# Graph layer with a routed feed-forward: the routing of the node blocks follows the update chunk by chunk, with roots by a power on GpSimd and slots counted inside partitions first

## The reference, cut to what matters

```
xn = layernorm(x)
msg = silu(layernorm(silu([xn[src], xn[dst], d2] @ mW1 + mb1)) @ mW2 + mb2)      # per edge
agg = segment_sum(msg, src)
x   = x + xn + silu([xn, agg] @ uW1 + ub1) @ uW2 + ub2 + mix(xn)                 # per node, the "update"
xm  = layernorm(layernorm(x)) * gamma + beta                                      # the rows that are routed
logits = xm @ Wr + br                                                             # 8 experts
top two experts of each row, weights = softmax over the two
x   = x + sum over the two of weight * (gelu(xm @ W1[e] + b1[e]) @ W2[e] + b2[e])
```

## Time and profile before

| | |
|---|---|
| median of 3 runs | 1701.5 us (1700.61 to 1703.49) |
| the profiled execution | 1703.06 us, of which the span is 1701.3 us |
| PE / DVE / ACT / POOL busy | 90% / 72% / 58% / 51% of the span |
| edge loop ends, update begins | about 1318 us from the start of the span |
| update | 1318 to 1391 us |
| routing and slots | 1391 to 1436 us |
| experts | 1446 to 1665 us |

### The profile page before, as it was taken

One profiled execution on the slowest core, in us unless ns is written; L12 is line 12 of the kernel. 1 busy time (PEld: TensorE's weight loads), 2 busy tenths in 40 slices (PEclk: granted clock), 3 DMA queues, 4 the chain that ended last, 5 costly groups with the idle time before them and its releaser, 6 DMA issues.

```text
span 1701.3 us, 34990 instructions
## 1 busy us (share of the span) xinstructions
PE 1530.8 (90%) x8931; PEld 1277.9 (75%) x8932; DVE 1218.8 (72%) x4343; ACT 983.3 (58%) x2126; POOL 865.8 (51%) x1201
## 2 busy tenths in 40 slices
PE   5799969899789999999999999999999874999992
PEld 2499946455568999999999999999898653677771
DVE  6788662566248989999899989899896359344442
ACT  1022112244138888888888888888887342556551
POOL 3088872000316666666666666666661002566651
PEclk8555569999789999999999999999999987999996
DMA  4700001100102222222222222222364024344447
GB/s 161 109 5 4 5 23 51 34 1 1 49 26 74 73 74 71 74 74 71 74 71 74 73 72 72 73 74 71 71 75 162 0 94 191 59 67 68 68 60 242
DMA packets 62950, 118.69 MB, mean 70 GB/s; under 512 B 19927, under 2 KB 40965, under 8 KB 62390
## 3 DMA queue, kind: packets, MB, share of 16 engines
q0 software_dynamic: 36560, 77.56, 19.7%
q1 hardware_dynamic: 25616, 37.26, 7.3%
q10 hardware_dynamic: 720, 3.20, 0.5%
HBM read 92.79 MB, written 25.18 MB: 69 GB/s over the span
## 4 chain that ended last, share of the span: by engine, by line
PE 83%; DVE 7%; ACT 4%; issue 3%; DMA 2%; DVEq 0%; SPq 0%; ACTq 0%; POOLq 0%
PE ps L903 12%; PE ps L664 9%; PE ps L995 6%; PE ps L883 5%; PE ps L712 5%; PE ps L792 5%; PE ps L873 5%; PE ps L870 4%; PE ps L865 4%; PE ps L866 4%; PE ps L756 3%; PE ps L718 3%; PE ps L893 2%; PE ps L1022 2%; PE ps L1021 1%
## 5 line engine op out<-in xcount | busy, mean ns | idle before, releaser
L612 POOL DMA_INDIRECT msg_t<-dst_table,stage_idx x448 | 446.7, 997 | 106.0 <-issue 45.0
L903 PE MATMUL ps<-msg_t,hot_t 128*125 128x256 f32 x896 | 241.5, 392 | 14.1 <-issue 7.4
L1118 ACT ACTIVATE msg1n_t<-msg_t,nw_b,nw_y 128x256 f32<-128x256 f32 x448 | 243.7, 598 | 0.0
L578 POOL DMA_INDIRECT sorted_edges<-sort_sb_t,chunk_to x112 | 156.5, 1398 | 100.6 <-DVE chunk_to L1307 66.8
L1135 ACT ACTIVATE msg_t<-msg_t 128x512 f32<-128x512 f32 x224 | 141.5, 632 | 101.2 <-DVE msg_t L1495 101.2
L865 PE MATMUL ps<-w_hi_t,msg1T_hi_t 128*128 128x256 f32 x672 | 198.6, 310 | 0.0
L866 PE MATMUL ps<-w_lo_t,msg1T_hi_t 128*128 128x256 f32 x672 | 180.0, 282 | 0.0
L903 PEld LDWEIGHTS ps<-msg_t,hot_t 128*125 128x125 f32 x896 | 151.3, 188 | 32.1 <-issue 9.6
L883 PE MATMUL ps<-src_hi_t,hotT_t 127*128 x448 | 160.7, 379 | 3.7 <-ACT hotT_t L1131 3.7
L1495 DVE TENSOR_TENSOR msg_t<-ps,msg_t 128x512 f32<-128x512 f32 x224 | 152.8, 682 | 3.1 <-PE ps L883 3.0
L870 PE MATMUL ps<-w_hi_t,msg1T_lo_t 128*128 128x256 f32 x672 | 153.8, 283 | 0.0
(11 more groups left out here) (324 smaller groups left out, 3806.4 us busy)
## 6 DMA issues: line engine op xcount, KB each, us to landing
w_sb_t<-in_L_ffn_W_dram SPq DMA_DIRECT2D x16, 512.0 KB, 8.0
msg_t<-dst_table,stage_idx POOLq DMA_INDIRECT x448, 2.8
res_t<-in_x_dram SPq DMA_DIRECT2D x1, 3125.0 KB
total<-zero_chunks_t SPq DMA_DIRECT2D x1, 3125.0 KB, 29.2
dst_table<-dst_stage SPq DMA_DIRECT2D x25, 125.0 KB
xm_table<-xm_t POOLq DMA_DIRECT2D x5, 625.0 KB, 8.8
total<-res_t SPq DMA_DIRECT2D x1, 3125.0 KB
sum_b_t<-total ACTq DMA_DIRECT2D x5, 625.0 KB, 11.4
```

Of the source, the lines that this page charges most:

```text
L578: pool.indirect_dma_start(out=sorted_edges, out_offset=bass.IndirectOffsetOnAxis(chunk_to[:, g, j:j + 1], 0), in_=sort_sb[:, g, j].rearran ...
L612: pool.indirect_dma_start(out=msg1[:, k, j, :], out_offset=None, in_=dst_table, in_offset=bass.IndirectOffsetOnAxis(stage_idx[:, half, q:q ...
L903: m = pe.matmul(bank(7, D, rows=NP), hot[:, (k - 8) % TURN, j, 0:NP].bitcast(F32), msg2[:, k % 2, j, :], start=(j == 0), stop=(j == G - 1))
L1118: m = A(msg1n[:, (k + 1) % 2, j, :], msg1[:, kk, j, :], ACT.Identity, bias=nw_b[:, kk, j:j + 1], scale=nw_y[:, kk, j:j + 1])
```

## The change

1. `aggT`, `hidT`, `x2T` move to the space of the edge weights, so that `xm` can be written while the update runs.
2. The statistics of a chunk are turned into 1/root on POOL, as a power of -0.5 (`spread_of` on DVE makes the base, `pool.tensor_tensor(..., ALU.pow)`), instead of ACT's square root and DVE's reciprocal.
3. DVE copies the raw logits of block t-3 out of PSUM ahead of block t (`raw_logits`); PE's `route(t)` waits for the copy of block t-1. Bias, scaled logits and top two of chunk c-2 come behind chunk c (`pick`).
4. ACT normalises the blocks of chunk c-2 behind chunk c (`copy_xm`), and POOL stores the first piece behind the root of chunk 4.
5. Slots: DVE scans `hot_k` itself, so that the place inside a partition and the partition's count of each expert (`row_n`) are known, and PE sums only 8 columns over the partitions.
6. PE waits for `w2_rest` only before the first product with W2.

```
+            for c in range(len(CH)):
+                T = slice(CH[c][0], CH[c][-1] + 1)
+                pool.wait_ge(var2_ok, c + 1)
+                pool.tensor_tensor(rstd[0:NP, T], rstd[0:NP, T], minus_half[0:NP, 0:len(CH[c])], ALU.pow).then_inc(sd2_ok, 1)
+                if c >= len(CH) - 3:
+                    store_rows(c - len(CH) + 3)
+            for g in range(3, 5):
+                store_rows(g)
...
             def route(t):
                 pe.wait_ge(x2T_sb, t + 1)
+                after(pe, logit_ok, t)
...
-            flat = hot_k[0:NP].rearrange("p e m -> p (e m)")
-            pe.matmul(bank(3, NE * KT, rows=NP), earlier[0:NP, 0:NP], flat, start=True, stop=True)
-            pe.matmul(bank(4, NE * KT, rows=NP), ones[0:NP, 0:NP], flat, start=True, stop=True).then_inc(route_ps, 1)
+            pe.matmul(bank(3, NE, rows=NP), earlier[0:NP, 0:NP], row_n[0:NP, :], start=True, stop=True)
+            pe.matmul(bank(3, NE, rows=NP, first=NE), ones[0:NP, 0:NP], row_n[0:NP, :], start=True, stop=True)\
+              .then_inc(route_ps, 1)
...
-            pe.wait_ge(w2_rest_ok, NE)
...
                     pe.wait_ge(shT_sb, m_ + 1)
+                    if isinstance(m_, int) and m_ == 0:
+                        pe.wait_ge(w2_rest_ok, NE)
...
+            def copy_xm(c):
+                act.wait_ge(rstd2_ok, c + 1)
+                for t in CH[c]:
+                    A(xm[0:NP, t, :], res[0:NP, t, :], ACT.Identity, bias=nbias[0:NP, t:t + 1], scale=rstd[0:NP, t:t + 1])\
+                        .then_inc(xm_ok, 1)
...
                 for t in blocks:
                     if t >= 1:
                         copy_x2(t - 1)
+                if c >= 2:
+                    copy_xm(c - 2)
             copy_x2(NB - 1)
-            act.wait_ge(var2_ok, 1)
-            A(rstd[0:NP], meanvar[0:NP, :, 1], ACT.Sqrt, bias=eps2_col[0:NP, :], scale=1.0 + EPS).then_inc(sd2_ok, 1)
...
+            copy_xm(len(CH) - 2)
+            copy_xm(len(CH) - 1)
...
+            def raw_logits(t):
+                if t >= 0:
+                    dve.wait_ge(logit_ps, t + 1)
+                    dve.tensor_copy(logits[R, t, :], bank(7, NE, rows=NP, first=t * NE)).then_inc(logit_ok, 1)
...
+            def pick(c):
+                blocks, n = CH[c], len(CH[c])
+                T = slice(blocks[0], blocks[-1] + 1)
+                dve.wait_ge(sd2_ok, c + 1)
+                dve.wait_ge(logit_ok, blocks[-1] + 1)
+                dve.scalar_tensor_tensor(nbias[R, T], meanvar[R, T, 0], -1.0, rstd[R, T], ALU.mult, ALU.mult)\
+                   .then_inc(rstd2_ok, 1)
...
                 for t in blocks:
+                    raw_logits(t - 3)
                     dve.wait_ge(upd_ps, t + 1)
...
+                if c >= 2:
+                    pick(c - 2)
+                if 1 <= c < len(CH) - 1:
+                    spread_of(c - 1)
...
+            spread_of(len(CH) - 2)
+            spread_of(len(CH) - 1)
+            for t in range(NB - 3, NB):
+                raw_logits(t)
+            pick(len(CH) - 2)
+            pick(len(CH) - 1)
...
-            hc = hot_c[R].rearrange("p e m -> p (e m)")
-            step(dve.tensor_copy(hc, bank(4, NE * KT, rows=NP)))
...
+            step(dve.tensor_tensor_scan(hp, hk, hk, 0.0, ALU.add, ALU.bypass))
+            st.did(dve.tensor_copy(row_n[R, 0:1], hot_p[R, 0:1, KT - 1]))
+            step(dve.tensor_tensor(row_n[R, 1:NE], hot_p[R, 1:NE, KT - 1], hot_p[R, 0:NE - 1, KT - 1], ALU.subtract))
+            dve.tensor_copy(nw_t[R, 0, 0:1], row_n[R, 0:1]).then_inc(hotk_ok, 1)
...
-            step(dve.tensor_tensor(hp, hp, hc, ALU.subtract))
-            step(dve.tensor_tensor(hp, hp, bank(3, NE * KT, rows=NP), ALU.add))
```

More of the change, by code:

```diff
@@ L202, in gps_layer @@
         msg2 = at("msg2_t", [128, 2, G, D], F32, "work", 30720)
[L205 to L206 removed]
+        aggT = [at(f"aggT{i}", [128, KD, 4, NP], F32, "weights", 4096 * i) for i in range(2)]
+        hidT = [at(f"hidT{i}", [128, KD, 4, NP], F32, "weights", 8192 + 4096 * i) for i in range(2)]
+        x2T = [at(f"x2T{i}", [128, KD, NP], F32, "weights", 16384 + 1024 * i) for i in range(2)]
         xm = at("xm_t", [128, NB, D], F32, "work")
[L209 to L210 removed]
         w1_sb = at("w1_sb_t", [128, NE, KD, HID], F32, "src_hi")
@@ L633, in _, with store_rows @@
                       allow_small_or_imprecise_dtypes=True).then_inc(token_ok, 1)
-            for g in range(5):
+            def store_rows(g):
                 pool.wait_ge(xm_ok, 5 * (g + 1))
@@ L1170, in _ @@
                         copy_x2(t - 1)
+                if c >= 2:
+                    copy_xm(c - 2)
             copy_x2(NB - 1)
-            act.wait_ge(var2_ok, 1)
-            A(rstd[0:NP], meanvar[0:NP, :, 1], ACT.Sqrt, bias=eps2_col[0:NP, :], scale=1.0 + EPS).then_inc(sd2_ok, 1)
-            act.wait_ge(rstd2_ok, 1)
-            for t in range(NB):
-                A(xm[0:NP, t, :], res[0:NP, t, :], ACT.Identity, bias=nbias[0:NP, t:t + 1], scale=rstd[0:NP, t:t + 1])\
-                    .then_inc(xm_ok, 1)
+            copy_xm(len(CH) - 2)
+            copy_xm(len(CH) - 1)
             act.wait_ge(gap_ok, 1)
@@ L1537, in add_hidden, with spread_of @@
                 m.then_inc(hid_pre, 1)
+            def raw_logits(t):
+                if t >= 0:
+                    dve.wait_ge(logit_ps, t + 1)
+                    dve.tensor_copy(logits[R, t, :], bank(7, NE, rows=NP, first=t * NE)).then_inc(logit_ok, 1)
+            def spread_of(c):
+                T = slice(CH[c][0], CH[c][-1] + 1)
+                st.join()
+                dve.tensor_scalar(rstd[R, T], meanvar[R, T, 1], 1.0 + EPS, EPS * EPS, ALU.mult, ALU.add).then_inc(var2_ok, 1)
+            def pick(c):
[5 more added lines that the diff above has]
+                   .then_inc(rstd2_ok, 1)
+                step(dve.tensor_tensor(logits[R, T], logits[R, T], rstd[R, T].unsqueeze(2).broadcast_to([NP, n, NE]), ALU.mult))
+                step(dve.tensor_tensor(logits[R, T], logits[R, T], logit0[R].unsqueeze(1).broadcast_to([NP, n, NE]), ALU.add))
+                for t in blocks:
+                    st.did(dve.max(top_v[R, t, :], logits[R, t, :]))
+                st.join()
+                for t in blocks:
+                    st.did(dve.max_index(top_e[R, t, :], top_v[R, t, :], logits[R, t, :]))
             dve.wait_ge(mixed_ok, NB)
@@ L1559, in _ @@
             st.join()
-            dve.tensor_copy(nw_t[R, 0, 0:1], meanvar[R, 0, 0:1]).then_inc(var2_ok, 1)
-            dve.wait_ge(sd2_ok, 1)
-            step(dve.reciprocal(rstd[R], rstd[R]))
-            dve.scalar_tensor_tensor(nbias[R], meanvar[R, :, 0], -1.0, rstd[R], ALU.mult, ALU.mult).then_inc(rstd2_ok, 1)
-            dve.wait_ge(logit_ps, NB)
-            step(dve.tensor_tensor(logits[R], bank(7, NB * NE, rows=NP).rearrange("p (t e) -> p t e", e=NE),
-                                   rstd[R].unsqueeze(2).broadcast_to([NP, NB, NE]), ALU.mult))
-            step(dve.tensor_tensor(logits[R], logits[R], logit0[R].unsqueeze(1).broadcast_to([NP, NB, NE]), ALU.add))
-            for t in range(NB):
-                st.did(dve.max(top_v[R, t, :], logits[R, t, :]))
-            st.join()
-            for t in range(NB):
-                st.did(dve.max_index(top_e[R, t, :], top_v[R, t, :], logits[R, t, :]))
+            spread_of(len(CH) - 2)
[4 more added lines that the diff above has]
+            pick(len(CH) - 1)
             st.join()
```

27 lines of the change are left out of this document (15 added, 12 removed).

## The result

The changed kernel takes 1710.9 us (median of 6 runs, 1706.8 to 1713.2) against 1701.9 for the kernel before in the same comparison (6 runs, 1700.2 to 1705.1): a ratio of 1.0050, with an interval from 1.0035 to 1.0065. It is slower by 9.0 us. The forecast was 4.3 us slower. The profiled execution took 1711.17 us, of which the span is 1709.4.

The account below looks back on a forecast made before the run. PE bounds the update, with ACT's copies of sums in its chain. 4.6 + 2.5 + 2.0 - 2.0 - 4.2 - 5.1 = -2.2 us, clock +6.5: 1707.4 us profiled, about 1706 median; 8-in-10 range 1696.5 to 1713.

Parts of the forecast that it names:

- ACT's copies ahead of the sums: Update: four normalising copies delay ACT's copy of sums by 1.52 us at three chunks, +4.6 us.
- Ahead of the last silu: End of update: four normalising copies behind chunk 5 delay the last block's silu, on which PE's product waits, +2.5 us.
- The raw logits: Update: PE's route waits for DVE's copy behind the additions, 0.5 us at the first block of chunks 1 to 4, +2.0.
- Last block to choice: From the last addition to `res` to `wtmp`: 9.4 us become about 7.0, plus 0.4 at the lower clock, -2.0.
- The power: POOL's power for 1/root: between 0.22 and 0.94 us, hidden; at the end up to about 1 us costs nothing.
- The rival of the slow power: Power on POOL takes 3 us and delays the last blocks' picking by 4 us: 1710 us, chance 0.05.
- The slots: Behind the choice: shorter matmuls -2.1, a copy and two additions gone -1.8, fewer small operations -0.3; together -4.2 us.
- The wait for `w2_rest`: Before the first expert tile: PE waits only for fetched rows, landing 3.7 us after issue; all 56 tiles shift, -5.1 us.
- the paragraph on transfers: W2 load starts about 9 us later, its list only some 3 later; with 12 us spare before, it stays covered.
- The rule on the shared port: First fetch beside DVE's work: could come up to one DVE operation later, making the -5.1 us term -3.9.
- The clock: Update: PE's longer stands lower TensorE's clock; two falls at 2.7 us and the last product at 1.1, +6.5.
- The rivals of a held clock and of a shorter stand that keeps PE warm: PE keeps 2.4 GHz: 1699.3 us, chance 0.22; full clock at the first expert tile too: 1697.4, chance 0.13.

Follow-up runs that it names:

- experiment 1: Changed kernel with all 25 normalising copies back behind the update on ACT: 1697.0 us against 1701.1 for the kernel before.
- the fillers: Changed kernel with eight unused products on PE behind the turning in chunks 3 to 5 and ahead of the last block: 1707.9 us, again 1705.8.
- experiment 2: Changed kernel with each chunk's first copy of raw logits ahead of DVE's two hidden-layer additions: 1704.1 us against 1701.1 for the kernel before.
- experiment 3: Kernel before with only the wait for `w2_rest` moved to the first product with W2: 1694.9 us against 1701.1 for the kernel before.
- experiment 5: Changed kernel with `res` stored into the totals in seven pieces during the update: 1703.4 us against 1700.2 for the kernel before.
- experiment 7: Changed kernel itself, without further edit, timed and profiled again: 1705.3 us against 1699.2 for the kernel before.

## Why the prediction was right, and where it was not

The direction, the range (1696.5 to 1713) and the mechanism held: copies in ACT's turn lengthen PE's stands, and TensorE's clock fell at some of them and at none where experiment 1 took them away or the fillers filled them; the fall at 1316.5 is the only one in the update at a stand that the change leaves alone. The amount was twice the forecast, and one term accounts for most of that. One sign on record came out the other way with it: PE's first expert transposition begins 8.57 us after the issue of the first fetch, not some 4.

- *ACT's copies ahead of the sums*, forecast +4.6: measured 1.42 + 1.42 + 2.06 = 4.9 (stands of 2.51, 2.51 and 2.53 against 1.09, 1.09 and 0.47). Ahead of the last silu, forecast +2.5: measured 2.83 - 0.43 = 2.4. Right in sum, and shown by experiment 1; the forecast had three equal parts of 1.52, but the third stand was 0.47 before, so it grew by more.
- *The raw logits*, forecast +2.0: measured 0.68 at each of four chunks, 2.7. The mechanism (additions ahead of the copy) is shown by experiment 2. The size was low because I set PE's route to start with the end of the copy and left out the hand-over, 0.15 us from 1351.39 to 1351.54.
- *Last block to choice*, forecast -2.0: measured -1.5. DVE's pickings cost 1.5, 1.5 and 0.9 us (1.6, 1.6, 1.0 in the forecast). The turns of PE's route and DVE's copy took 2.7 us (copies at 1408.40, 1409.72 and 1411.05) where I had 1.6 and 0.4 for the lower clock. The 1.4 us of draining that the forecast weighs could not have made this gain larger: the old stage is measured, 9.40 us with all that it holds.
- *The power*, forecast nothing from a bound of 0.22 to 0.94: it took 1.01 to 1.05 on 125 x 4, above the upper bound, and cost nothing in the changed kernel, at the edge of the cover that the forecast named. The rival of the slow power falls.
- *The slots*, forecast -4.2: -4.15, and the same within 0.02 us in every version that has them.
- *The wait for `w2_rest`*, forecast -5.1: measured -0.3. **This is the step that failed**, and with it the paragraph on transfers. The term took the landing of 3.7 us from fetches beside which the store was ending or over. The paragraph followed the load of W2 as far as ACT's rounding, which did stay covered (done at 1438.1, some 7 us ahead of the first `w2_rest`), and forgot what stands behind that load on SP's queue. The fetch came 5.6 us nearer to the end of the update (45.7 to 40.1), into a store whose traffic ebbs some 47 to 48 us behind it (about 1438 before, 1453 after). Experiments 3 and 5 show both halves: alone the edit gives -4.9, and with the store out of the way the changed kernel gets it too.
- The rule on the shared port (the Trainium skill, SBUF — State Buffer, section Who interferes with whom), by which the fetch could come up to a DVE operation later, agrees in kind with the rows: in the kernel before the fetches beside `w_rest` took 1.74 to 1.98 us to issue and landed after 3.6 to 3.8, those behind it 0.94 to 0.99 and 2.8 in the median. The page limits the rule to GpSimd instructions that read SBUF; the fetch reads its row numbers there. But the 3.7 of the term was taken from fetches beside `w_rest`, so that cost was in it already, and the -3.9 would have counted it twice: experiment 3 has 3.97 us from issue to transposition. That DVE's operations are what lengthens the issue was not tried.
- *The clock*, forecast +6.5: worked out as the length of the update less 71.59, less the 7.3 of ACT and the 2.7 of the raw logits where they apply, it cost 8.9 us in the first profile (1.7 of them at the unchanged first hidden layer), 5.5 in experiment 5, 5.8 in experiment 2 and 2.6 in experiment 7. The forecast lies among them; that the same stand costs 1.7 us in one execution and nothing in the next was not foreseen. Why is open. The medians of the changed kernel, 9 and 6 us above before, don't show it: their ratios, 1.0050 and 1.0046, agree. The rivals of a held clock and of a shorter stand that keeps PE warm fall: the clock fell in each of these profiles, and was low at the first expert tile (3.78 us for the first product with W1).

The sum: 4.9 + 2.4 + 2.7 - 1.5 - 4.15 - 0.3 = about +4.0 us without the clock, where the forecast had -2.2, and the clock's 2.6 to 8.9 on top, against 9.0 and 6.1 us between the medians. The 4.8 us of the failed term are most of the 6.2 between the two sums. That the total still lies in the range is in part luck: no rival and no bound of the forecast allowed for this term.

## What to carry to other kernels

Before work is moved into a stage because its engine is mostly idle there, look at what stands behind it in that engine's own order: four copies of 0.5 us ahead of the one copy that PE waits for cost 7 us and the clock's share, where all 25 behind the stage had cost nothing, and one copy in each gap cost 0.6. When a wait is removed, list every transfer that is open at the new, earlier time, the ones queued behind others on SP too: the next wait can be a transfer that nobody had waited for, as here. And take a releaser named at a wait for two semaphores as a guess until one of them has been moved.

## What the runs showed that was not expected

- A stand of PE of 2.51 us, the same to 0.01 us, sometimes brings the clock down to 1.2 GHz and sometimes not, in different executions and within one (hidden layers of 5.31 and 3.62 us, experiment 7). A single profile misjudges such a cost by several microseconds.
- A store on SP's queue delays a gather that POOL issues on another queue: 8.0 to 8.6 us to landing in seven profiles where the store was open, 3.5 to 3.8 in seven where it was over or ending, though the store alone takes only 0.30 of the DMA engines' time.
- POOL's power takes 1.01 to 1.05 us for 125 x 4 values and 0.59 for 125 x 1, where a product of 128 x 4 takes 0.22.
- 24 transpositions of 2.81 us, followed by a stand of 1.92, kept the clock up where one stand of 5.2 us didn't.
